# Layer 0: seven pieces of a weight matrix are loaded through the queue of GpSimd instead of SyncE's

## The reference

```
x = x + L0_ffn(L0_cond(x))     # 8 low-rank adapters of rank 16, mixed by a softmax router
x = x + L1_ffn(L1_cond(x))     # x @ kernel (1024 x 1024) + bias + low-rank terms, mixed by a gate
x = x + L2_ffn(L2_cond(x))     # x @ base_W.T + the 2 best of 28 experts of rank 8
x = x + L3_ffn(L3_cond(x))     # x @ W.T + b + a routed low-rank term
```

## Time and profile before

| | |
|---|---|
| median of 3 runs | 1902.27 us (1899.55 to 1908.01) |
| profiled execution | 1907.9 us, of which the span is 1906.1 us |
| PE busy | 1778.4 us, 93% |
| DVE, ACT, POOL busy | 839.0, 665.4 and 58.1 us |
| SP's queue (q1) | 173.35 MB |
| POOL's queue (q0) | 2.13 MB |
| 16 DMAs of the dense kernel | 256 KB each, median 7.0 us from issue to landing |

### The profile page before, as it was taken

The page is one execution under the profiler, slowest core; times in us unless marked ns, Lnnn a source line. Parts: engine busy times, 40 slices in busy tenths (PEclk is TensorE's granted clock), DMA queues, the critical chain, the costliest instruction groups (busy, mean ns, idle before and its releaser), DMA issues.

```text
span 1906.1 us, 25849 instructions
## 1 busy us (share of the span) xinstructions
PE 1778.4 (93%) x9128; PEld 1476.4 (77%) x9128; DVE 839.0 (44%) x2329; ACT 665.4 (35%) x1237; POOL 58.1 (3%) x99
## 2 busy tenths in 40 slices
PE   5888998978999999999899999999989999999995
PEld 4777777767888888887688888888777888888873
DVE  5154555554333334355543444434564333333327
ACT  2355555433333333334432323323253333332310
POOL 2000000010000000001000000000102000000000
PEclk9799999968999999999999999999998999999996
DMA  6657667438333233314322222222241223222218
GB/s 123 129 127 166 141 151 156 116 86 105 83 80 91 55 91 80 86 46 134 110 76 65 66 75 59 78 64 56 69 117 45 64 77 84 75 80 70 65 43 331
DMA packets 227625, 181.76 MB, mean 95 GB/s; under 512 B 176184, under 2 KB 187672, under 8 KB 227294
## 3 DMA queue, kind: packets, MB, share of 16 engines
q1 hardware_dynamic: 222142, 173.35, 35.8%
q10 hardware_dynamic: 2640, 5.26, 0.9%
q0 software_dynamic: 2768, 2.13, 0.8%
HBM read 108.34 MB, written 42.99 MB: 79 GB/s over the span
## 4 chain that ended last, share of the span: by engine, by line
PE 63%; issue 23%; DVE 5%; SPq 3%; DMA 3%; ACT 2%; POOL 1%; POOLq 0%; DVEq 0%; ACTq 0%
PE ps L1000 54%; PE ps L1815 3%; SPq L1352 3%; DMA filt<-filt 2%; PE ps L1134 2%; PE ps L1086 1%; DVE w_lo L1483 1%; DMA raw<-in_L_ffn_W 1%; DVE x_last L1970 1%; DVE filt L775 0%; POOL limes_rep L1895 0%; PE ps L2027 0%; ACT w_hi L1479 0%; ACT filt L441 0%; PE ps L1835 0%
## 5 line engine op out<-in xcount | busy, mean ns | idle before, releaser
L1000 PE MATMUL ps<-xp_hi,filt 128*128 128x512 f32 x1024 | 336.2, 410 | 18.0 <-DMA filt<-filt 15.8
L1000 PE MATMUL ps<-w_hi,y_hi 128*128 128x512 f32 x768 | 312.5, 407 | 0.0
L1000 PE MATMUL ps<-w_hi,y_lo 128*128 128x512 f32 x768 | 305.4, 398 | 0.0
L1000 PE MATMUL ps<-w_lo,y_hi 128*128 128x512 f32 x768 | 304.7, 397 | 0.0
L1000 PEld LDWEIGHTS ps<-xp_hi,filt 128*128 128x128 f32 x1024 | 192.5, 194 | 62.7 <-DMA filt<-filt 15.2
L764 DVE SCALAR_TENSOR_TENSOR xp_lo<-ps,mods_pair,xp_hi 128x512 fp32r<-128x512 f32 x128 | 96.3, 752 | 276.6 <-ACT xp_hi L431 272.6
L431 ACT ACTIVATE xp_hi<-ps,mods_pair 128x512 fp32r<-128x512 f32 x128 | 88.1, 689 | 360.0 <-PE ps L1000 360.0
L1000 PE MATMUL ps<-xp_lo,filt 128*128 128x512 f32 x512 | 206.3, 403 | 0.0
L447 ACT ACTIVATE y_nat<-ps,mods_pair 128x512 f32<-128x512 f32 x128 | 99.6, 778 | 213.3 <-PE ps L1000 213.2
L1000 PEld LDWEIGHTS ps<-w_lo,y_hi 128*128 128x128 f32 x768 | 145.4, 189 | 35.3
L1000 PEld LDWEIGHTS ps<-w_hi,y_hi 128*128 128x128 f32 x768 | 146.0, 190 | 31.2
(11 more groups left out here) (317 smaller groups left out, 2879.1 us busy)
## 6 DMA issues: line engine op xcount, KB each, us to landing
x_in<-x_state SPq DMA_DIRECT2D x96, 256.0 KB, 3.9
x_res<-x_state SPq DMA_DIRECT2D x48, 512.0 KB, 3.9
x_state<-x_res SPq DMA_DIRECT2D x46, 512.0 KB, 2.9
filt<-filt SPq DMA_DIRECT2D x128, 128.0 KB, 2.7
filt<-filt SPq DMA_DIRECT2D x128, 96.0 KB, 2.5
raw<-in_x SPq DMA_DIRECT2D x16, 512.0 KB, 5.3
x_res<-in_x SPq DMA_DIRECT2D x16, 512.0 KB, 4.3
x_state<-raw SPq DMA_DIRECT2D x16, 512.0 KB, 3.8
```

The source lines that it names most:

```text
L1000: ins = nc.tensor.matmul(out, st[x0], mv[x1], start=first and t == 0, stop=last and t == 2, **kw)
```

## The change

Pieces 1 to 7 of the dense kernel are issued by POOL. Piece 0 stays with SP. Pieces 1 to 7 get a semaphore of their own, `kernel_more`, so the wait in `split_kernel_act` is written in two cases. In POOL's list piece 1 stands behind the weights of layer 1's convolutions and ahead of the loads of edge sets 1 and 2; pieces 2 to 7 stand in a loop behind these. The wait for `kernel_dve` goes with each load.

```diff
@@ sp_step
             if more and load_next:
                 sp_load_x(sp, l, n + 3)
-            if l == 0 and load_next and j == 1:
-                load_kernel(sp, i + 2)
             if more:
                 sp_shift_filter(sp, l, n + 2)
@@ load_kernel
             for h in range(2):
-                sp.dma_start(kernel_in[:, h:KB:2], kernel_cols[h, e]).then_inc(s["kernel_loaded"], 16)
+                sp.dma_start(kernel_in[:, h:KB:2], kernel_cols[h, e]).then_inc(s["kernel_loaded" if is_zero(e) else "kernel_more"], 16)
@@ split_kernel_act
-            act.wait_ge(s["kernel_loaded"], 32 * e + 32)
+            if is_zero(e):
+                act.wait_ge(s["kernel_loaded"], 32)
+            else:
+                act.wait_ge(s["kernel_more"], 32 * e)
@@ block.sync
                 if l == 0:
                     load_mixed(sp, 0)
-                    load_kernel(sp, 1)
@@ block.gpsimd
                 pool_load_edge(gp, l, 0)
                 if l + 1 < LAYERS:
                     load_cond_weights(gp, l + 1)
+                if l == 0:
+                    load_kernel(gp, 1)
                 for g in range(1, EDGE_SETS):
                     pool_load_edge(gp, l, g)
+                if l == 0:
+                    with gp.Fori(2, GROUPS) as e:
+                        load_kernel(gp, e)
                 if l + 1 < LAYERS:
                     load_cond_rest(gp, l + 1)
```

More of the change, by code:

```diff
@@ L235, in build @@
             dve_mp dve_g dve_t dve_y dve_x dve_b dve_l dve_p dve_end dve_k dve_z dve_zt dve_o dve_e
-            x_loaded e_loaded chain""".split()
+            x_loaded e_loaded chain kernel_more""".split()
         s = {n: sem(n) for n in names}
```

## The result

The changed kernel takes 1911.24 us (median of 16 runs, 1906.29 to 1918.10) against 1903.91 us before (median of 16, 1898.17 to 1913.11). The ratio is 1.0031, with a 95% interval from 1.0016 to 1.0046: 3 to 9 us more, 5.9 at the middle. The forecast was +3.2 us, 1905.5, and a change of less than 0.5%; so it proved. The measured median lies 5.7 us above 1905.5 and 1.2 us above 1901 to 1910, the range that the prediction gave the forecast itself; it lies inside the wide range of 1889 to 1915. Against the kernel before, +5.9 us is inside the forecast's -1 to +7.6. The profiled execution has a span of 1910.2 us, 4.1 us more than before.

The account below looks back on a forecast made before the run. The prediction took PE, busy 93% of the span, as the bound, so only PE's waits count. 6.2 - 3.0 = +3.2 us on a median of 1902.3 gave 1905.5 us, own range 1901 to 1910, wide range 1889 to 1915.

Parts of the forecast that it names:

- Part 1: Start of layer 0's loop: edge set 1 queues behind piece 1 on POOL, delaying e_x and PE by +6.2 us (5.2 to 7.6).
- Part 2: End of six passes: pieces 2 to 7 leave SP's queue, so the shift gains 0.5 us each, -3.0 us (0 to -14.4).
- +7.8: In the passes: POOL's traffic could cost SP's DMAs 1.3 us, six times.
- -6: The gain subtracted from 5.2 to give the lower end, -1, of the forecast's own range.
- third rival: In the passes: POOL's packets push between those of the shift, 1.3 us six times; +14.0 in all, 1916 us, chance 0.12.
- Part 3: Small things, each 0: SP's saved issue time, edge set 2 behind set 1, later landing of pieces, the loop on POOL.
- The shift gets free of the piece: In the passes: the shift lands as without a piece, -14.4 us of waits and -8.4 of clock; 1886 us, chance 0.17.
- The edge load crawls: Start of the loop: edge loads take 14.4 us to land, a stall of 16.5; 1919 us, chance 0.10.
- POOL's packets push between: In the passes: POOL's packets delay the shift's by 1.3 us six times, +7.8; +14.0 in all, 1916 us, chance 0.12.

Follow-up runs that it names:

- e1: The changed kernel with edge set 1 issued ahead of piece 1 on POOL; ratio to the kernel before 1.0010 (1906.87 us), again 1.0011 (1906.99 us).
- e2: The changed kernel with only piece 1 on POOL, ahead of edge set 1, and pieces 2 to 7 back on SP; ratio 1.0041, 1911.30 us.
- e8: e1 with pieces 1 to 7 held on POOL for the event that lets SP issue the first filter's shift; ratio 0.9958, 1896.48 us.
- e3: The kernel before without the loads of pieces 2 to 7, the splits running on what lies in the buffer; ratio 0.9889, 1883.97 us.
- e4: The kernel before with each piece's load moved behind the filter's shift in SP's list; ratio 0.9899, 1887.30 us.

## Why the prediction was right

**Part 1, the wait at e_x: right in mechanism and size.** Forecast e_x at 115.7, measured 115.25; forecast wait of PE 10.4 us, measured 9.4 twice. The issues of the piece took 1.52 us together (forecast 1.4), the edge issues 1.53 (1.50), and the landing was 3.0 us where I had taken 4.0. The row of the same queue and order, 3.1 us at 407 us, was the right one, and my allowance above it was not needed. The stall is 5.2 us by PE's wait and 5.3 by the time from ACT's first split (3.74 to 9.06 us; 8.90 in the second execution), and not 6.2 (111.65 + 4.0 - 109.54 gives 6.1, and the upper end 7.5 and not 7.6). That 115.25 lies so near 115.7 is partly luck: the second edge load went out some 0.8 us later than forecast, half of it because piece 0 had landed later, and made up for that by its shorter landing. Moving edge set 1 back ahead of the piece restores the wait of 4.2 us and the 3.74 us of before (e1, both executions), and piece 1 alone brings the loss (e2): this step is shown.

**Part 2, the passes: the size was right, the reason for it only half.** I forecast -3.0 us with bounds from -14.4 to +7.8 and put it near zero because the DMA share was already above 1. The 0.5 us a pass behind the -3.0 was a choice that no run showed; the zero end would have been nearer. In the profiled pair the loop gave back 1.6 us, and in the other four executions with pieces on either queue ahead of the shift its length scatters from 257.5 to 260.6, around the 258.8 of before. So the gain is not told from zero, and the copy that PE waits for landed after 6.1 to 6.5 us where 5.5 to 6 was forecast. The sum of the two parts, +3.2, was too low by this term and too high by 0.9 in the other. The forecast's own range was also narrower than its terms: its -6 has no row behind it, and the +7.8 was left out of its upper end. The mechanism that I gave for "no gain" was that the engines serve both queues in turn. What the trace shows is service in the order of issue, x, then piece, then shift. With that order the packets of the two queues hardly meet, which fits the third rival's failing, and a second queue did not help while the piece was issued first.

The Trainium skill ("DMA: Bandwidth & Descriptors", Issuing engines are not separate DMA queues) says that another issuer saves only issue time; the trace agrees: the copy that PE waits for landed after 6.1 to 6.5 us with two queues and after 6.0 to 6.4, once 7.6, with one. Its rule of turn-taking between queues, a packet at a time (Queues, rings and completion order), does not describe the microseconds from 146 to 149, when no packet of POOL's queue moved beside those of x, nor the one from 150, when SP's queue moved one. At 149 and 151, the changeovers, both moved. In e8 both queues moved packets within a microsecond, which is nearer to it. The measurement decides: here the rule doesn't give the time of the shift.

**Part 3: the zeros held.** No wait of ACT for pieces 1 to 7 appears, with a landing of 6.5 to 7.0 us for pieces 2 to 7, nor any of DVE for a DMA of edge set 2.

**The rivals.** "The shift gets free of the piece" was priced at 14.4 us of waits and 8.4 of clock, 22.8 together; with the bytes gone (e3) the loop is 22.5 us shorter, so the price was right and only the condition was not met. In e4, which keeps the loads and swaps the order, it is met nearly. "The edge load crawls" is out, 3.0 us and not 14.4. "POOL's packets push between" is out: the waits for the shift sum to 14.7 to 16.8 us in the four executions with all pieces on POOL ahead of the shift, and to 15.8 before.

**What stays open.** The measured loss, 0.31% and 0.26%, is 5 to 6 us, which the stall of 5.3 us fills, and with edge set 1 first 0.1% remains, which is not told from zero. A candidate is seen in the profiles: SP's small loads and the residual now follow straight on piece 0, and in two of the seven profiled executions that have them there, ACT waited 7.6 or 7.8 us for piece 0; in the other five it was 5.5 to 5.9, and 5.6 in each of the three that don't. Two microseconds in two executions of seven are 0.6 us on average, less than the 2 us in question. Holding these loads back was not tried, so this is argued and not shown.

## What to carry to other kernels

When a load is moved to another engine's list, look first at what stands behind it there: a wait that was harmless in one list delayed two tiny loads that had gone out 76 us early in the other. When a copy is late behind a bulk load that was issued ahead of it, try the order of issue before the queue. The piece had time to spare and the shift none; two lines moved, which swap them in the same queue, gave -1.0% where the change of queue gave +0.3%.

## What the runs showed of the hardware

In the changed kernel the DMA engines served bulk transfers of two queues in the order of issue: from 146 to 149 us not one packet of POOL's queue was served beside SP's load of x, at 150 us POOL's 69 packets stood against 1 of SP's, and the shift followed; in the changeovers at 149 and 151 both queues moved (47 and 17 packets, 130 and 74). Where piece and shift were issued within 1.5 us (e8), both moved packets in the same microseconds. POOL's queue began to move packets 1.5 us after the issue when the engines were free (110.16 to 111.65), and some 4 us after it behind x (145.03 to 149). The piece also moves in other packets on POOL: 0.24 MB in 69 packets at 150 us, 3.5 KB each, where SP's queue took 0.22 MB in 441 packets for it, 0.5 KB each (from 145 to 146 us before). The first filter's copies landed no differently for it (6.1 to 6.5 us). With the piece in its own queue SP took 1.92 us to issue the third copy of the shift, and 0.63 with the piece in POOL's. And six idle spells of 2 to 3.6 us on PE cost more than themselves: 13.5 us of waiting less came with 22.5 us of loop less, the granted clock over the loop rising from 0.95 to 0.99 and PE's busy time falling by 8.8 us for the same matmuls.
